# Second attention: queries by halves with the context in one bank, two bank pairs for scores alone, three single banks for scan, maxima and outputs

## The reference

```python
q = (x @ wq).reshape(b, s, 32, 8).transpose(0, 2, 1, 3)
k = (x @ wk).reshape(b, s, 8, 8).transpose(0, 2, 1, 3)
v = (x @ wv).reshape(b, s, 8, 8).transpose(0, 2, 1, 3)
q = _apply_rope(q, cos, sin)
k = _apply_rope(k, cos, sin)
k = jnp.repeat(k, 4, axis=1)
v = jnp.repeat(v, 4, axis=1)
scores = jnp.einsum('bhqd,bhkd->bhqk', q, k) / 8 ** 0.5
scores = jnp.where(causal[None, None], scores, -jnp.inf)
probs = jax.nn.softmax(scores, axis=-1)
out = jnp.einsum('bhqk,bhkd->bhqd', probs, v)
return out.transpose(0, 2, 1, 3).reshape(b, s, 256) @ wo
```

## Time and profile before

| | us |
|---|---|
| three runs | 1960.10, 1962.92, 1960.93 (median 1960.93) |
| the profiled execution | 1962.14 |
| its span, first to last instruction | 1960.1 |
| mean granted TensorE clock | 0.951 |
| the stage's units: scans alone | 1188.0 to 1212.6 |
| scans beside scores, 15 times | 1212.6 to 1733.6 |
| scores alone | 1733.6 to 1757.9 |

### The profile page before, as it was taken

One profiled execution on the slowest core, in us unless ns is written; L12 is line 12 of the kernel. 1 busy time (PEld: TensorE's weight loads), 2 busy tenths in 40 slices (PEclk: granted clock), 3 DMA queues, 4 the chain that ended last, 5 costly groups with the idle time before them and its releaser, 6 DMA issues. The chain is left out here.

```text
span 1960.1 us, 43323 instructions
## 1 busy us (share of the span) xinstructions
PE 1651.5 (84%) x14612; PEld 1021.4 (52%) x14612; DVE 1382.8 (71%) x2658; ACT 1136.6 (58%) x2158; POOL 666.2 (34%) x756
## 2 busy tenths in 40 slices
PE   2899999999999999999448375888888888883897
PEld 1577777777777777777324232333333333332454
DVE  4487777877777778777675566777777777737564
ACT  4566666666666666666456521555565555566454
POOL 1655555545554555554021150121111211123011
PEclk9899999999999999999869687999999999996899
DMA  4322111211121111111000101000000000001000
GB/s 126 87 51 52 45 40 45 51 37 45 40 51 48 43 45 46 45 43 27 1 1 1 35 3 22 9 11 15 9 16 11 13 14 9 9 2 64 1 22 22
DMA packets 53104, 61.79 MB, mean 32 GB/s; under 512 B 11345, under 2 KB 32018, under 8 KB 53010
## 3 DMA queue, kind: packets, MB, share of 16 engines
q1 hardware_dynamic: 53010, 60.55, 12.7%
HBM read 18.57 MB, written 2.10 MB: 11 GB/s over the span
## 5 line engine op out<-in xcount | busy, mean ns | idle before, releaser
L1604 DVE TENSOR_REDUCE a_mx<-psum 128x2 f32<-128x1024 f32 (+3 forms) x384 | 359.1, 954 | 122.3 <-PE psum L1502 92.2
L1564 ACT ACTIVATE a_prob_r<-psum 128x1024 f32<-128x1024 f32 (+3 forms) x256 | 219.0, 864 | 145.1 <-PE psum L1518 144.0
L1498 PE MATMUL psum<-a_kd,a_qp 128*128 128x512 f16 (+3 forms) x768 | 192.7, 336 | 49.0 <-DVE a_mx L1604 26.1
L528 POOL TENSOR_TENSOR a_swp<-a_swp,a_sin 128x512 f32<-128x512 f32 x128 | 163.1, 1275 | 162.2 <-DMA a_swp<-a_lin 162.2
L884 DVE TENSOR_REDUCE a_nmax<-psum 128x1 f32<-128x1024 f32 (+7 forms) x256 | 191.3, 748 | 1.0 <-PE psum L599 1.0
L532 POOL TENSOR_TENSOR a_rope<-a_swp,a_cosd 128x512 f32<-128x512 f32 x128 | 164.1, 1282 | 12.4 <-POOL a_swp L528 4.8
L224 POOL TENSOR_TENSOR x<-x,y (+1 forms) x64 | 54.4, 879 | 319.5 <-ACT y L196 319.5
L756 ACT ACTIVATE a_prob_big<-psum,a_nmax 128x1024 f32<-128x1024 f32 (+3 forms) x128 | 121.8, 952 | 68.5 <-DVE a_nmax L884 65.0
L879 DVE TENSOR_TENSOR a_pt_lo_big<-psum,a_pt_hi_big 128x512 f16<-128x512 f32 (+3 forms) x256 | 138.7, 583 | 31.0 <-ACT a_pt_hi_big L751 30.3
L1518 PE MATMUL psum<-a_qf,a_kd 32*128 32x512 f16 (+3 forms) x768 | 124.4, 334 | 41.8 <-DVE a_mx L1604 38.6
L1564 ACT ACTIVATE a_prob_l<-psum 128x1024 f32<-128x1024 f32 (+3 forms) x128 | 89.8, 705 | 116.3 <-PE psum L1518 116.2
(11 more groups left out here) (260 smaller groups left out, 4661.4 us busy)
## 6 DMA issues: line engine op xcount, KB each, us to landing
a_swp<-a_lin SPq DMA_DIRECT2D x256, 128.0 KB, 2.3
a_qp<-a_q_part SPq DMA_DIRECT2D x192, 16.0 KB
a_kd<-a_k_part SPq DMA_DIRECT2D x192, 16.0 KB
x<-_attn_hidden_states_dram SPq DMA_DIRECT2D x4, 512.0 KB, 5.8
a_w_raw<-in_L_attn_Wq_dram SPq DMA_DIRECT2D x16, 128.0 KB, 2.2
a_w_raw<-in_L_attn_Wk_dram SPq DMA_DIRECT2D x16, 128.0 KB, 2.3
a_w_raw<-in_L_attn_Wv_dram SPq DMA_DIRECT2D x16, 128.0 KB, 2.3
a_wo_raw<-in_L_attn_Wo_dram SPq DMA_DIRECT2D x1, 2048.0 KB
```

What stands on the lines that cost most here:

```text
L528: pool.tensor_tensor(swp[:, ch, :], swp[:, ch, :], sin[:, (i % 2) * BANK:(i % 2 + 1) * BANK], ALU.mult).then_inc(sin_done, 1)
L1498: last = pe.matmul(c.psum[:, pair_of(k) + h, 0:n], qp[:, w % 3, t * P:(t + 1) * P], kd[:, w % 3, 2 * pair + h, a:e], start=True, stop=not ...
L1564: act.activation(prob_at(u, kt, a)[:, 2 * pair:2 * pair + 2, a % BANK:a % BANK + e - a], c.psum[:, pair_of(k):pair_of(k) + 2, 0:e - a], AC ...
L1604: dve.tensor_reduce(mx[:, t, 2 * pair:2 * pair + 2, a // BANK], c.psum[:, pair_of(k):pair_of(k) + 2, 0:e - a], AX.X, ALU.max).then_inc(sca ...
```

## The change

Queries are worked by halves: `KQ` runs over all key tiles of the left half, then over all of the right, and both halves accumulate their context in bank 4, so the right half's first piece waits until ACT has copied the left half out. Scan jobs take one bank instead of two: `QK` has 38 jobs, with four heads together where a piece has 128 keys, two where it has 256, and one head where it has 384 or 512. Scores alternate between two pairs, banks 0 to 3, and wait for the exp two jobs back; scans, maxima and outputs go through banks 5 to 7 in turn and wait for the third of their kind back (`work_free`). The probabilities have one ring of four pieces. The due times of scans follow their columns, and the left half's outputs come at 12.6 instead of 19.6.

```diff
         QK = []
         for t in range(TB):
             for p0 in range((t * P) // BANK + 1):
-                QK += [(t, p0 * BANK, min((p0 + 1) * BANK, (t + 1) * P), pair) for pair in range(2)]
+                n = min(BANK, (t + 1) * P - p0 * BANK)
+                per = J if n == P else BANK // n if n <= BANK // 2 else 1
+                QK += [(t, p0 * BANK, p0 * BANK + n, j, per) for j in range(0, J, per)]
         KQ = []
-        for t in range(TB):
-            for a, e in spans(t * P, S):
-                KQ += [(t, a, e, pair) for pair in range(2)]
-        NJ, NC = len(QK), len(KQ) // 2
-        NU, LAG = B * G1, 3
+        for half in range(CB):
+            for t in range(TB * (half + 1) // CB):
+                KQ += [(t, max(t * P, half * BANK), (half + 1) * BANK, pair) for pair in range(2)]
+        NS, NJ, NC = len(QK), len(KQ), len(KQ) // 2
+        LAST_OF = (TB // CB - 1, NC - 1)
+        NU, LAG, LEAD = B * G1, 3, 1.17
         N_DMA = 6 * J
 
         def in_order(u):
 
             timed = [(i + 0.5, "X", i) for i in range(NJ)] if u >= 0 else []
             if u + 1 < NU:
-                timed += [(0.87 * i, "S", i) for i in range(NJ)]
-                timed += [(0.87 * (QK.index((3, 0, BANK, 1)) + 1.7), "M", 0), (0.87 * (NJ + 0.7), "M", 1)]
+                cost = [sum((e - a) * per for _, a, e, _, per in QK[:i]) / (2 * BANK) for i in range(NS + 1)]
+                half = 1 + max(i for i in range(NS) if QK[i][0] == 3)
+                timed += [(LEAD * cost[i], "S", i) for i in range(NS)]
+                timed += [(LEAD * cost[half] + 1.4, "M", 0), (LEAD * cost[NS] + 0.6, "M", 1)]
             if u >= 0:
-                timed += [(19.6, "O", 0)]
+                timed += [(2 * LAST_OF[0] + 1 + LAG + 2.6, "O", 0)]
             if u >= 1:
                 timed += [(4.6, "O", 1)]
             return [(kind, u - 1 if (kind, i) == ("O", 1) else u + 1 if kind in "SM" else u, i) for _, kind, i in sorted(timed)]
...
-            prob_l, prob_r = asb("prob_l", [P, 2, J, BANK]), asb("prob_r", [P, 3, J, BANK])
+            prob = asb("prob", [P, 4, J, BANK])
...
-            def pair_of(k):
-
-                return (0, 2, 6)[k % 3]
-
-            def prob_at(u, kt, a):
-
-                if a < BANK:
-                    return prob_l[:, (4 * u + kt) % 2, :, :]
-                return prob_r[:, (8 * u + kt) % 3, :, :]
-
-            def last_piece(u, kt, a):
-
-                return NC * u + next(n for n in range(NC) if KQ[2 * n][0:2] == (kt, a)) + 1
+            def pair_of(u, i):
+                return 2 * ((NJ * u + i) % 2)
+
+            def work(job):
+                return c.psum[:, 5 + WORK.index(job) % 3, :]
+
+            def prob_at(u, i):
+                return prob[:, (NC * u + i // 2) % 4, :, :]
...
-                    def slot_free(k):
-
-                        if k >= 3:
-                            before = JOBS[k - 3]
-                            pe.wait_ge({"X": exp_done, "S": scan_done, "M": qf_ready, "O": att_ready}[before[0]], COUNT[before])
-
-                    def scan(k, w, i):
-                        t, a, e, pair = QK[i]
-                        n, edge = e - a, e == (t + 1) * P
+                    def work_free(job):
+
+                        n = WORK.index(job)
+                        if n >= 3:
+                            before = WORK[n - 3]
+                            pe.wait_ge({"S": scan_done, "M": qf_ready, "O": att_ready}[before[0]], COUNT[before])
...
+                    def scan(w, i):
+                        t, a, e, j0, per = QK[i]
+                        n, edge, to = e - a, e == (t + 1) * P, work(("S", w, i))
+                        work_free(("S", w, i))
                         pe.wait_ge(loaded_qk[w % 3], 16 * N_DMA * (w // 3 + 1))
-                        for h in range(2):
-                            last = pe.matmul(c.psum[:, pair_of(k) + h, 0:n], qp[:, w % 3, t * P:(t + 1) * P],
-                                             kd[:, w % 3, 2 * pair + h, a:e], start=True, stop=not edge)
-                        if edge:
-                            for h in range(2):
-                                last = pe.matmul(c.psum[:, pair_of(k) + h, n - P:n], c.ident_b[:, :], c.mask_qk[:, :],
+                        for j in range(per):
+                            last = pe.matmul(to[:, j * n:(j + 1) * n], qp[:, w % 3, t * P:(t + 1) * P],
+                                             kd[:, w % 3, j0 + j, a:e], start=True, stop=not edge)
+                            if edge:
+                                last = pe.matmul(to[:, (j + 1) * n - P:(j + 1) * n], c.ident_b[:, :], c.mask_qk[:, :],
                                                  start=False, stop=True)
                         last.then_inc(s_made, 1)
...
+                        wait(pe, exp_done, NJ * u + i - 1)
...
-                            wait(pe, o_ready, 2 * (u - 1) + a // BANK + 1)
+                            wait(pe, o_ready, 2 * u + a // BANK)
                         for j in range(J):
-                            last = pe.matmul(c.psum[j * R:(j + 1) * R, 4 + a // BANK, a % BANK:a % BANK + e - a],
-                                             vg[:, u % 2, kt, :], prob_at(u, kt, a)[:, j, a % BANK:a % BANK + e - a],
+                            last = pe.matmul(c.psum[j * R:(j + 1) * R, 4, a % BANK:a % BANK + e - a],
+                                             vg[:, u % 2, kt, :], prob_at(u, 2 * n)[:, j, a % BANK:a % BANK + e - a],
                                              start=(kt == 0), stop=(kt == (e - 1) // P))
...
+                    def exponent(u, i):
                         kt, a, e, pair = KQ[i]
                         act.wait_ge(x_made, NJ * u + i + 1)
                         if pair == 0:
-                            ring, per, used = (2, 4, 4 * u + kt) if a < BANK else (3, 8, 8 * u + kt)
-                            if used >= ring:
-                                of, kt_of = divmod(used - ring, per)
-                                act.wait_ge(ctx_made, last_piece(of, kt_of, max(kt_of * P, BANK if per == 8 else 0)))
-                        act.activation(prob_at(u, kt, a)[:, 2 * pair:2 * pair + 2, a % BANK:a % BANK + e - a],
-                                       c.psum[:, pair_of(k):pair_of(k) + 2, 0:e - a], ACT.Exp, scale=SCALE).then_inc(exp_done, 1)
+                            wait(act, ctx_made, NC * u + i // 2 - 3)
+                        act.activation(prob_at(u, i)[:, 2 * pair:2 * pair + 2, a % BANK:a % BANK + e - a],
+                                       c.psum[:, pair_of(u, i):pair_of(u, i) + 2, 0:e - a], ACT.Exp, scale=SCALE).then_inc(exp_done, 1)
 
                     def output(u, half):
-                        act.wait_ge(ctx_made, NC * u + (NC if half else last_piece(0, 3, 3 * P)))
+                        act.wait_ge(ctx_made, NC * u + LAST_OF[half] + 1)
                         wait(act, o_made, 2 * (u - 2) + half + 1)
-                        act.activation(o_sb[:, u % 2, half * BANK:(half + 1) * BANK], c.psum[:, 4 + half, :], ACT.Copy).then_inc(o_ready, 1)
-
-                    for k, (kind, u, i) in enumerate(JOBS):
+                        act.activation(o_sb[:, u % 2, half * BANK:(half + 1) * BANK], c.psum[:, 4, :], ACT.Copy).then_inc(o_ready, 1)
+
+                    for kind, u, i in JOBS:
                         if kind == "X":
-                            exponent(k, u, i)
-                            if i == 17:
+                            exponent(u, i)
+                            if i == 2 * LAST_OF[0] + 1 + LAG:
                                 output(u, 0)
-                            if i == 2 and u >= 1:
+                            if i == LAG - 1 and u >= 1:
                                 output(u - 1, 1)
...
-                    def scan(k, w, i):
-                        t, a, e, pair = QK[i]
-                        dve.wait_ge(s_made, NJ * w + i + 1)
-                        dve.tensor_reduce(mx[:, t, 2 * pair:2 * pair + 2, a // BANK], c.psum[:, pair_of(k):pair_of(k) + 2, 0:e - a],
+                    def scan(w, i):
+                        t, a, e, j0, per = QK[i]
+                        dve.wait_ge(s_made, NS * w + i + 1)
+                        dve.tensor_reduce(mx[:, t, j0:j0 + per, a // BANK],
+                                          work(("S", w, i))[:, 0:per * (e - a)].rearrange("p (j n) -> p j n", j=per),
                                           AX.X, ALU.max).then_inc(scan_done, 1)
-                        if e == (t + 1) * P and pair == 1:
-                            dve.wait_ge(scan_done, NJ * w + i + 1)
+                        if e == (t + 1) * P and j0 + per == J:
```

More of the change, by code:

```diff
@@ L1431, in attention_1 @@
         for kind in "XSMO":
-            for n, job in enumerate(j for j in JOBS if j[0] == kind):
+            for n, job in enumerate(one for one in JOBS if one[0] == kind):
                 COUNT[job] = n + 1
+        WORK = [job for job in JOBS if job[0] != "X"]
```

(30 more changed lines are left out.)

8 lines of the change are left out of this document (4 added, 4 removed).

## The result

The changed kernel takes 1904.41 us (median of four runs, 1904.03 to 1904.82) against 1961.93 beside it: ratio 0.971, 95% interval 0.969 to 0.972, 57.5 us faster. The forecast was 1917, so the sign and the place were right and the gain was some 13 us larger than its sum. Measured times are medians of executions at the usual clock; one execution of the grouped order, 2207 us at a granted clock of 0.735, is left out of its median.

The account below looks back on a forecast made before the run. No engine was full; scans and scores waited on each other in a shared ring. Units going from 34.7 to 31.6 us, times 15, gave -46.5, first unit +2.0: -44.5 on 1962.14, predicted 1917 us, range 1890 to 1950.

Parts of the forecast that it names:

- The place and the mechanism: Second attention's 15 middle units: scans and scores wait on each other in one three-pair ring; separating them saves 46.5 us.
- the third bank's argument: Work ring: three queued scans, 2.1 us of DVE work, cover PE's longest stretch without a scan, 0.32 + 1.00 us.
- DVE's +2.4 us a unit: Scan reductions: 38 single-bank jobs replace 24, raising DVE from 26.0 to 28.4 us a unit; +0.7 if consecutive reductions overlap.
- PE's own need, 29.8: Sum of PE's matmuls, masks and switches in one unit: 29.8 us, against 30.2 busy in the windows.
- The price of a switch: PE changing between scans, scores and contexts: 0.11 to 0.15 us each, 57 of them some 7 us a unit.
- 31.6 us a unit: Middle units: later engine's time over three stretches, 32.2 us, less 0.6 for overlapping reductions, against 34.7 before.
- 0.8 at the second maxima: End of each unit: PE waits 0.8 us until DVE has emptied its ring after the last scans.
- Rival A: Middle units: PE becomes sole bound, DVE wholly hidden, 29.8 to 30.6 us a unit, 1895 us; chance 0.17 (and below).
- Rival B: Scan reductions: each of 38 keeps a 0.27 us handoff, 38.7 us a unit, 2023 us; chance 0.11.
- Rival C: Score jobs: each stands 0.13 us waiting for its pair's exp, 1963 us, half of it 1940; chance 0.10.
- First unit: First unit, scans alone: DVE's +2.4 us is bare, less overlap, so +2.0 us.
- Last unit: Last unit, scores alone, set by ACT: two pairs instead of three cost 0, up to +1.0 us.

Follow-up runs that it names:

- grouped order: Changed kernel with a key tile's two score jobs adjacent, their context piece behind, then three or four scans; 36 switches a unit instead of 58: 1898.72 us.
- one ring: Changed kernel with scans, scores, maxima and outputs put back into one ring of three bank pairs; halves, single-bank scans and order stay: 1986.35 us.
- two banks: Changed kernel with scans, maxima and outputs in a ring of two single banks instead of three, bank 7 unused: 1972.54 us.
- short reductions: Changed kernel with each scan's reduction reading only the first half of its piece's keys; PE's work, jobs and waits stay: 1869.37 us.
- short exps: Changed kernel with each exp handling only the first half of its columns (pieces of 128 whole), probabilities' buffers zeroed once at the start: 1900.53 us.
- no mask in the scans: Changed kernel without the causal mask in the scans, 32 small mask matmuls a unit left out on PE: 1890.35 us.
- The run without halves: Changed kernel with scores in the old order, context in banks 4 and 5, two single work banks and two score pairs: 1971.92 us.
- bf16 context: Changed kernel with probabilities and values of the context held in bf16 instead of f32, so the output is coarser: 1852.17 us.
- later scans: Changed kernel with the scans' due times stretched, factor 1.27 for 1.17: 1906.65 us.

## Why the prediction was right, and where its steps were off

- **The place and the mechanism: right, but I gave the credit to the wrong half of it.** I said that scans and scores stood for each other in a shared ring. Separating them without the third work bank is worth 1.2 us a unit (36.3 to 35.0); the third bank behind it, 4.3 (35.0 to 30.7). The changed kernel has five slots where before and the one ring had three, and no run has a shared ring with more slots: how much of the gain is separation and how much is the number of slots is open. The prediction had the third bank's argument (three scans ahead cover the longest stretch without one) but no price for it, and my expectation for two banks shows that I would have priced it at 6 to 31 us instead of 68. Had the change had two banks, I would have forecast a gain where there was a loss.
- **DVE's +2.4 us a unit: mis-sized.** The instruction times were right to 0.01 us, their overlap was not: reductions of 512 columns overlap by 0.044 each, and DVE's busy time a unit stayed 26.0 (the reductions' 7.7 us more are offset in its small instructions, which take 22.0 instead of 25.5 at L1614 and L1616, and in overlap). The prediction had the +0.7 as its lower bound, from one pair in the timeline, and the reductions' own sum rose by 7.7 / 15 = 0.5. The row to price an engine's share by is the busy sum of a group, not the mean of one. By the Trainium skill (Perfetto Trace Analysis, Optimizing Scalar/DVE Operations) a DVE instruction on PSUM carries some 125 ns of access overhead. Here 14 x 15 more of them added 7.7 us of busy time, 0.037 each, and the measurement decides.
- **PE's own need, 29.8: near.** The run with short reductions has 29.0, with no gap between PE's records. The price of a switch was in line with the grouped run: 0.126 us of busy time each. By the Trainium skill (TensorEngine Tiling (Array Packing), Key Properties) a change of tiling mode drains TensorE; the grouped run is in line with it, at those 0.126 us. One aside of the prediction does not come out: with DVE as the bound at 28.4 us a unit, its own base and first unit give 1870 us, not near 1880 (-6.3 x 15 + 2.0 on 1962.14).
- **31.6 us a unit against 30.7.** The sum took, stretch by stretch, the later of two engines, with DVE at 9.3 + 16.2 + 3.7 = 29.2 where it needs 26.0. The ring does not let PE and DVE run free either, so what stands above PE's 29.0 is coupling, at least 1.7, which the sum held only as 0.8 at the second maxima. There PE waits 3.4 us in 15 units, 0.2 each. Two errors of opposite sign, then: DVE too dear, the coupling too cheap. Their net is the 0.9 us a unit, 13.7 in all; that it is no larger, and leaves the forecast as near as 13 us, is in part luck.
- **Rival A (PE alone, 1895 us)** was 9 us from the result, nearer than my 1917, but its reading, DVE wholly hidden, is what the short reductions refute.
- **Rival B (0.27 us of handoff at each reduction, 2023 us)** fell: 42.0 / 570 = 0.07. With two banks it is (52.5 + 27.1) / 570 = 0.14, near the 0.165 from which the prediction let it decide, and that run is indeed slower than before.
- **Rival C** fell, by the short exps, though the waits put down to exps, 34.8 us, passed the 20 that I had named for the forecast.
- **First unit: +2.0 forecast, +0.8 measured,** the same overlap. **Last unit: 0 to +1.0 forecast, +2.3 measured.** ACT's last output copy there starts 22.0 us after the mark before (1733.55 to 1755.55), 22.9 in the runs with short reductions (1639.95 to 1662.89) and with no mask in the scans (1660.13 to 1683.08), 24.3 in the changed kernel's (1674.41 to 1698.68). The run without halves, with the old order and two pairs, has 22.8 (1743.93 to 1766.76). So some 0.9 comes with two pairs in place of three, and 1.3 with a drop of the clock, below. The pairs' part is not isolated: the one ring, with three pairs and the new order, has 25.4 (1756.55 to 1781.90), but at a granted clock of 0.87.

## What to carry to other kernels

Two engines that hand over through a short ring in a fixed order can stand for each other long before either is full; here a ring of two and a ring of three were different kernels, 68 us apart. Counting the work that the ring holds against the longest stretch in which the other engine does something else was not enough to price this: some 40 us stayed where that count said the third bank was hardly needed. Splitting a reduction to fit more slots in the same memory cost DVE 0.04 us of busy time a piece here, not the 0.16 that its duration's intercept suggests. When both engines were within 15% of the path, taking work from one paid only in part (12.9 us of 17.1 of PE's busy time, 52.9 of 70.4 with the bf16 context), and reordering one traded against the ring.

## What the hardware showed that I had not expected

In the last unit PE is idle for a larger share than in the 15 before (4.9 of 26.3 us against 9.8 of 460.6), and the granted clock falls from full to half and back within 6 us (windows of the changed kernel):

```profile
1676.00:1678.00 2.00, 1.44 (x18) 0.44 (x14) 0.00 (x0) 2.00 (x3) 0.98 (x3) 1.00 0.04 8
1678.00:1680.00 2.00, 1.43 (x12) 0.33 (x10) 0.00 (x0) 2.00 (x4) 0.92 (x3) 0.64 0.00 0
1680.00:1682.00 2.00, 2.00 (x16) 0.73 (x8) 0.00 (x0) 0.12 (x1) 0.51 (x2) 0.51 0.00 0
1682.00:1684.00 2.00, 1.98 (x25) 0.58 (x24) 0.55 (x2) 1.59 (x4) 1.03 (x3) 1.00 0.00 0
```

Ahead of the fall PE was busy 1.44 of 2.0 us. A 512-column context piece at 1679.07 takes 1.93 us instead of 1.06, four transposes 1.11 instead of 0.66: 1.3 us lost, and ACT stands for it. It is not in every profile: the runs with short reductions and with no mask in the scans were granted 1.00 over their last unit, the grouped order 0.94 with 0.50 at the lowest (1671 to 1673), the one ring and the later scans 0.87. What decides it no run shows. With the bf16 context, where PE has less to do, the last unit runs at a mean of 0.55, near the lower of the two levels, 1.2 GHz, though in the loop, with PE busy 93%, it stays at 0.97. That lower clock cost little there: ACT's last output copy starts 22.8 us after the mark (1620.46 to 1643.26), against 22.9 in the f32 runs at full clock.
